# Pre-norm attention and feed-forward layer: PSUM copy of the second layer norm's transposes moved from VectorE to ScalarE

## The reference, cut to what matters

```python
# x: [32, 2048, 1024] float32; one core has 4 of the 32
x = x + attention(layernorm(x))        # 16 heads of 64, low-rank q and kv, causal softmax
h = gelu(layernorm(x) @ w1 + b1)       # w1: [1024, 4096], erf form of gelu
x = x + h @ w2 + b2                    # w2: [4096, 1024]
```

## Time and profile before

| | |
|---|---|
| time, median of 2 runs | 11111.08 us (11088.33 and 11133.84) |
| profiled execution, its own time | 10802.03 us |
| span of its slowest core (core 3) | 10800.3 us |
| spans of all cores | 10786.9 to 10800.3 us |
| busy on core 3: PE, DVE, ACT, POOL | 5923.8, 4608.4, 2902.2, 205.2 us |

### The profile page before, as it was taken

How to read it: one execution, slowest core, us unless ns; L and a number is a source line. 1 busy time by engine, 2 the same in 40 slices (tenths; PEclk the granted TensorE clock), 3 DMA queues, 4 the chain that set the end, 5 groups by cost and what they waited for, 6 DMA issues and landing times.

```text
span 10800.3 us, 104032 instructions; the slowest of 8 cores (10786.9 to 10800.3 us)
## 1 busy us (share of the span) xinstructions
PE 5923.8 (55%) x29865; PEld 2726.9 (25%) x29865; DVE 4608.4 (43%) x16081; ACT 2902.2 (27%) x4830; POOL 205.2 (2%) x592
## 2 busy tenths in 40 slices
PE   3344545534455554344545533445464578777788
PEld 1122222212222222122222221222222233333333
DVE  4554545555555554555555545555454011001111
ACT  2322222232232322233223223222222222332221
POOL 0000000000000000000000000000000100000000
PEclk5555555555555555555555555555555799999999
DMA  1000000000000000000000000000000410111110
GB/s 20 18 2 19 2 19 2 18 3 20 18 3 10 10 2 18 20 2 18 3 18 3 1 20 18 3 19 2 16 1 21 87 37 23 39 38 40 39 33 29
DMA packets 67323, 192.35 MB, mean 18 GB/s; under 512 B 9192, under 2 KB 9232, under 8 KB 66768
## 3 DMA queue, kind: packets, MB, share of 16 engines
q0 software_dynamic: 36864, 83.90, 4.0%
q1 hardware_dynamic: 29904, 101.79, 2.8%
HBM read 168.89 MB, written 67.11 MB: 22 GB/s over the span
## 4 chain that ended last, share of the span: by engine, by line
PE 41%; DVE 33%; issue 14%; ACT 8%; DVEq 1%; DMA 1%; POOL 1%; ACTq 0%; SPq 0%; POOLq 0%
DVE PT L873 7%; DVE S_sb L740 7%; PE ps_c L889 7%; PE pt_y L863 5%; PE pt_x L863 5%; PE ps_b L1136 4%; PE ps_a L1136 4%; PE ps_c L1113 4%; PE ps_d L1113 4%; DVE mcol L757 2%; DVE qn_tok L595 2%; DVE kst L621 2%; DVE x_buf L826 2%; DVE qst L524 2%; DVE S_sb L750 2%
## 5 line engine op out<-in xcount | busy, mean ns | idle before, releaser
L787 ACT ACTIVATE P_A<-S_sb,negm,rstdq_win 128x256 bf16<-128x256 f32 (+15 forms) x512 | 662.1, 1293 | 3452.3 <-PE pt_y L863 2766.4
L889 PE MATMUL ps_c<-PT,vst 128*64 128x512 bf16 (+3 forms) x2560 | 734.8, 557 | 1387.8 <-DVE PT L873 1387.8
L727 PE MATMUL ps_s<-kst,qst 128*128 128x512 bf16 (+3 forms) x1280 | 651.4, 525 | 421.6 <-DVE S_sb L740 297.9
L873 DVE COPY PT<-pt_y 128x1024 bf16<-128x1024 bf16 (+2 forms) x640 | 374.3, 585 | 1092.3 <-PE pt_y L863 1092.3
L873 DVE COPY PT<-pt_x 128x1024 bf16<-128x1024 bf16 (+1 forms) x640 | 405.4, 633 | 996.6 <-PE pt_x L863 996.6
L787 ACT ACTIVATE P_B<-S_sb,negm,rstdq_win 128x256 bf16<-128x256 f32 (+15 forms) x512 | 662.2, 1293 | 536.5 <-DVE negm L770 535.3
L740 DVE TENSOR_SCALAR_CACHE_REDUCE S_sb<-ps_s 128x512 f32<-128x512 f32 (+2 forms) x1152 | 673.9, 614 | 299.5 <-PE ps_s L727 295.6
L1148 DVE TENSOR_SCALAR ybf<-ps_a,b2col 128x512 bf16<-128x512 f32 x64 | 48.0, 751 | 1370.9 <-PE ps_a L1136 1370.9
L889 PEld LDWEIGHTS ps_c<-PT,vst 128*64 128x64 bf16 x2560 | 205.4, 128 | 1691.4 <-issue 1691.4
L609 PE MATMUL pt_y<-id_bf,qn_tok 128*64 128x128 bf16 x1024 | 132.1, 310 | 882.9 <-DVE qn_tok L595 882.9
L1113 PE MATMUL ps_c<-Xn2T,w1b 128*128 128x512 bf16 x2048 | 508.4, 393 | 24.3 <-DMA w1b<-W 20.3
(11 more groups left out here) (202 smaller groups left out, 8819.5 us busy)
## 6 DMA issues: line engine op xcount, KB each, us to landing
x_buf<-x SPq DMA_DIRECT2D x64, 512.0 KB, 7.3
x2s<-x_buf POOLq DMA_DIRECT2D x64, 512.0 KB, 5.1
x_buf<-x2s SPq DMA_DIRECT2D x64, 512.0 KB, 6.0
y<-x_buf SPq DMA_DIRECT2D x64, 512.0 KB, 4.3
xln<-x POOLq DMA_DIRECT2D x64, 256.0 KB, 4.2
xln<-x2s POOLq DMA_DIRECT2D x64, 256.0 KB, 3.7
w1b<-W POOLq DMA_DIRECT2D x32, 256.0 KB, 9.7
w2b<-W POOLq DMA_DIRECT2D x32, 256.0 KB, 8.5
```

Source lines behind the costliest of these rows:

```text
L727: P.step("pe", lambda t, h=h, qt=qt, off=off, w=w, ps=ps: t.matmul(ps[:, 0:w], qstack[h][:, qt * 128:(qt + 1) * 128], kstack[h][:, off:off ...
L787: P.step("ac", lambda a, P_sb=P_sb, po0=po0, klen=klen, slot=slot, spar=spar, rc=rc: a.activation(out=P_sb[:, po0:po0 + klen], in_=S2[spar ...
L873: P.step("dv", lambda v, par=par, qt_min=qt_min: v.tensor_copy(PT2[par][:].rearrange("p (h f) -> p h f", f=512) [:, :, qt_min * 128:512], ...
L889: P.step("pe", lambda t, hi=hi, grp=grp, v0=v0, par=par, qt_min=qt_min, j=j, nj=nj: t.matmul(ps_c[hi * HD:(hi + 1) * HD, qt_min * 128:512] ...
```

## The change

The copy of `pt_x` to `Xn2T2` is recorded for ScalarE as an activation with the function Copy and no scale or bias tensor, in place of the VectorE copy. It is at the same place of the Python code, so it now stands in ScalarE's queue behind the normalisation of its own chunk (line 1033) and ahead of the first step of the next chunk (line 993). The semaphore that says that the block is ready, and that frees `pt_x` for the next transposes, is now ScalarE's (`ac_f`) and no longer VectorE's (`dv_f`). Amount of data, layout and all else stay.

```diff
-                    P.step("dv", lambda v, tc=tc, s_=s_: v.tensor_copy(
-                        Xn2T2[s_ % 2][:].rearrange("p (c f) -> p c f", f=512)
+                    P.step("ac", lambda a, tc=tc, s_=s_: a.activation(
+                        out=Xn2T2[s_ % 2][:].rearrange(
+                            "p (c f) -> p c f", f=512)
                         [:, :, tc * 128:(tc + 1) * 128],
-                        pt_x[:].rearrange("p (c f) -> p c f", f=128)),
+                        in_=pt_x[:].rearrange("p (c f) -> p c f", f=128),
+                        func=AF.Copy),
                         wait=[pe_ft]
                         + (r_Xn2Tb[s_ % 2].waits() if tc == 0 else []),
-                        inc=dv_f)
-                    r_ptx.set(dv_f)
+                        inc=ac_f)
+                    r_ptx.set(ac_f)
...
-                ln2_marks[s_] = dv_f.n
+                ln2_marks[s_] = ac_f.n
...
-                            wait=([(dv_f, xn2T_ready),
+                            wait=([(ac_f, xn2T_ready),
```

## The result

| | before | after |
|---|---|---|
| median of all runs | 10802.68 us (10 runs) | 10842.86 us (13 runs) |
| profiled execution | 10802.03 us | 10838.65 us |
| ratio | | 1.0038, 95% interval 1.0027 to 1.0049 |

The change costs 40 us (0.38%), within what was called no change; 43 us had been forecast. But the forecast's time, 11154 us with 11088 to 11233 as its range, is 311 us too high, because it was added to the median of the two runs known then, 11111 us. In some executions of each of these kernels the cores of one die show a lower granted clock and end up to 3.6% later, so the ratios leave out the longest of them, and where such executions pull a median up, the single fastest run is read.

The account below looks back on a forecast made before the run. TensorE was taken to idle at 14 block boundaries behind the layer norm's chain on ScalarE and GpSimd. 48 exposed copies x 0.90 = 43 us, added to the 11111 us median, gave 11154 us, range 11088 to 11233.

Parts of the forecast that it names:

- what was called no change: Whole kernel: a difference of about 2%, what a measurement can tell from no change; chance of ending within it 0.93.
- the clock above: TensorE's granted clock at the 14 block boundaries: a longer turn shifts its return, taken as 0 with 8 us either side.

Follow-up runs that it names:

- e3: The changed kernel with each copy made a second time on ScalarE after the first has ended; fastest run 10889.86 us, median 10937.33 us, ratio 1.0132 to the kernel before.

## What to carry to other kernels

An instruction that waits for another engine belongs on a queue where nothing ready stands behind it. Before moving one, list what is recorded behind it on the new engine: its cost is its length times the number of places where the next instruction is urgent, and far more (269 us here, for 40) once buffers would let that engine run ahead. Relieving an engine wins nothing where the work taken off it is hidden: VectorE is busy 43% of the whole span and has a third of the chain of waits there, but the 64 copies had no place on it. Moving the layer norm's chain itself under other work gave 367 us.

And where the timed runs and the profiled execution disagree by per cents, and only two runs are known, forecast the difference from the trace and keep both levels in the range.

## What was not expected of the hardware

The granted clock that is recorded for a core did not set its time in the attention stage, nor the length of its matmuls. In the kernel before, the first 1000 us of core 0 and of core 3 (columns as in the earlier trace rows):

```profile
0.00:1000.00 1000.00, 391.89 (x2253) 198.76 (x2268) 518.47 (x1960) 289.20 (x602) 13.73 (x38) 1.00 0.06 16
0.00:1000.00 1000.00, 396.79 (x2270) 198.57 (x2270) 520.01 (x1965) 290.27 (x605) 14.17 (x39) 0.51 0.07 16
```

The clock is 1.00 on one and 0.51 on the other, but a matmul takes 174 and 175 ns on the mean. The changed kernel's core 7 likewise had a mean of 0.57 up to 8320 us against 0.50 in the earlier trace rows, with TensorE busy 4011.6 against 4011.1 us:

```profile
0.00:8320.00 8320.00, 4011.60 (x20649) 1850.67 (x20649) 4353.87 (x15369) 2258.52 (x3841) 67.88 (x140) 0.57 0.04 11
```

Whether the record or the reading of it is at fault there stays open. In the feed-forward stage the clock and the times do go together (see the clock above).

ScalarE starts an activation 0.10 us before the recorded end of the one before, unless it waits for that one's completion; then it starts 0.10 us after it (e3). In a chain of dependent steps on ScalarE that would be 0.2 us a step, an estimate from e3's rows alone. The Trainium skill, page "ScalarE: Activation LUTs", section "What ACT_TABLE_LOAD costs", gives the overlap as about 93 ns, and the trace agrees (0.10 us).
